# The router's logits in the last stage of a four-stage transformer kernel: the router's columns as the stationary operand, the rows streamed past them, the result copied and turned back

## The reference

```python
logits = jnp.einsum('bsd,ed->bse', x, router_w) + router_b
probs = jax.nn.softmax(logits, axis=-1)
weights = jnp.max(probs, axis=-1)
top1 = jnp.argmax(probs, axis=-1)
y_all = jnp.einsum('bsd,eod->bseo', x, expert_w) + expert_b
y = jnp.take_along_axis(y_all, top1[:, :, None, None], axis=2)[:, :, 0, :]
out = y * weights[:, :, None]
```

## Time and profile before

| | us |
|---|---|
| median of 3 runs | 3087.24 (3087.1 to 3090.45) |
| the profiled execution, its own time | 3084.65 |
| its span | 3082.2 |
| router part of the last stage | some 103, from 2809 to 2912 |
| table and fill rows | some 25, to 2937 |
| tiles | some 145, to the end |

### The profile page before, as it was taken

One profiled execution on the slowest core, in us unless ns is written; L12 is line 12 of the kernel. 1 busy time (PEld: TensorE's weight loads), 2 busy tenths in 40 slices (PEclk: granted clock), 3 DMA queues, 4 the chain that ended last, 5 costly groups with the idle time before them and its releaser, 6 DMA issues. The chain is left out here.

```text
span 3082.2 us, 85861 instructions
## 1 busy us (share of the span) xinstructions
PE 2883.8 (94%) x27000; PEld 2603.0 (84%) x27000; DVE 2280.3 (74%) x6196; ACT 1874.3 (61%) x6944; POOL 1553.2 (50%) x1813
## 2 busy tenths in 40 slices
PE   2999999889999999997999999999989999997777
PEld 2888888689999999996999999999978888886656
DVE  5888888877777777776777777777778888886533
ACT  3888888755555555554444444444378888885443
POOL 1666565566666666665222222222246666563645
PEclk9999999999999999998999999999999999996588
DMA  6000000010000000000000000000010000001243
GB/s 214 15 17 14 17 17 14 2 61 11 10 10 12 10 10 10 10 12 23 25 10 12 12 10 10 10 10 11 1 53 17 14 17 15 15 8 36 94 131 115
DMA packets 55924, 86.12 MB, mean 28 GB/s; under 512 B 6784, under 2 KB 42625, under 8 KB 55042
## 3 DMA queue, kind: packets, MB, share of 16 engines
q1 hardware_dynamic: 47204, 65.69, 6.9%
q0 software_dynamic: 6528, 16.92, 1.5%
q10 hardware_dynamic: 2080, 2.10, 0.2%
HBM read 57.25 MB, written 28.48 MB: 28 GB/s over the span
## 5 line engine op out<-in xcount | busy, mean ns | idle before, releaser
L642 ACT ACTIVATE L_probs<-bank,L_neg_max 128x128 f32<-128x128 f32 x2048 | 716.8, 403 | 138.0 <-DVE L_neg_max L714 137.4
L642 ACT ACTIVATION_READ_ACCUMULATOR L_probs<-bank,L_neg_max 128x1 f32 x2048 | 498.2, 243 | 0.0
L720 DVE COPY L_probsT<-bank 128x512 f32<-128x512 f32 x512 | 352.7, 689 | 141.2 <-PE bank L537 82.3
L1778 ACT ACTIVATE M_inter<-bank 128x512 f32<-128x512 f32 x256 | 153.3, 599 | 438.0 <-PE bank L69 387.1
L67 PE MATMUL bank<-W_hi,M_nT_hi 128*128 128x384 f32 (+1 forms) x1024 | 369.9, 361 | 7.6 <-DVE M_qkv L1404 4.5
L714 DVE TENSOR_REDUCE L_neg_max<-bank 128x4 f32<-128x512 f32 x512 | 327.5, 681 | 36.8 <-PE bank L514 36.8
L69 PE MATMUL bank<-W_lo,M_nT_hi 128*128 128x384 f32 (+1 forms) x1024 | 346.6, 338 | 0.0
L68 PE MATMUL bank<-W_hi,M_nT_lo 128*128 128x384 f32 (+1 forms) x1024 | 346.0, 338 | 0.0
L524 PE MATMUL bank<-constants,L_probs 128*128 128x128 f32 x2048 | 326.0, 283 | 13.0 <-ACT L_probs L642 9.8
L1837 DVE TENSOR_TENSOR M_inter_lo<-M_inter,M_inter_hi 128x512 fp32r<-128x512 f32 x256 | 206.7, 808 | 168.8 <-ACT M_inter_hi L1779 159.7
L67 PE MATMUL bank<-W_hi,M_inter_hi 128*128 128x256 f32 x1024 | 290.4, 284 | 11.7 <-DVE M_inter_lo L1837 10.9
(11 more groups left out here) (344 smaller groups left out, 9232.4 us busy)
## 6 DMA issues: line engine op xcount, KB each, us to landing
L_ctx_in<-in_ctx SPq DMA_DIRECT2D x64, 256.0 KB, 2.6
M_tile<-M_sorted SPq DMA_DIRECT2D x72, 130.0 KB
raw_weights<-in_weights SPq DMA_DIRECT2D x2, 4096.0 KB, 13.5
hs<-M_hs SPq DMA_DIRECT2D x64, 128.0 KB, 1.7
M_hs<-hs SPq DMA_DIRECT2D x32, 256.0 KB, 2.7
x_all<-in_x SPq DMA_DIRECT2D x6, 1024.0 KB, 8.0
M_sorted<-M_fill SPq DMA_DIRECT2D x16, 130.0 KB
x_all<-in_x ACTq DMA_DIRECT2D x2, 1024.0 KB, 14.9
```

Of the source, the lines that this page charges most:

```text
L642: last = act.activation(probs[:, k % UNITS, i, :], score_bank[u][:, i, :], ACT.Exp, bias=neg_max[:, u, i:i + 1], scale=-1.0, accum_out=sum ...
L720: dve.tensor_copy(probsT[:, k % 2], pT_ps[k % UNITS]).then_inc(pT_ready, 1)
L1778: act.activation(inter[:, e % 2], up_bank[e % 2], ACT.Gelu).then_inc(M.inter_ready, 1)
```

## The change

Router products are turned round. `dot_router(p)` now loads the router's columns (16, or 8 for the remainder rows) and streams the 256 tokens of the pair past them, for each half of the features: four products, into [16, 256] of bank 6 or 7. ScalarE copies that into `dotsT` (`keep_dots`). A new step `fold(p)` multiplies, for each of the two sequences, dotsT's 128 tokens (stationary, 16 rows, plain fp32) with a constant [16, 8] of two stacked identities (`fold`, eight columns more in the constants): this turns the dots back to [128 tokens, 8] and adds the two eights. VectorE's first addition of a group falls away. On TensorE `fold(p - 1)` stands between `turn_n(p + 1)` and `dot_router(p)`. The exponential moves from p = 8, 12, ... to p = 9, 13, ... in ScalarE's queue (the first stays at p = 4). `round_n(p)` and `choose(g)` wait for folds where they waited for products.

```diff
--- before.py
+++ after.py
@@ -143,6 +143,7 @@
         "rank": np.tile(np.arange(E, 0, -1), (P, 2, 1)),
         "minus_half": np.full((P, 2), -0.5),
         "one": np.ones((P, 1)),
+        "fold": np.tile(np.eye(E), (P // E, 1)),
         "euler": np.full((P, 2, E), np.e),
     }
 
@@ -1987,7 +1988,8 @@
         sem = lambda name: signals.sem(f"{L}_{name}")
         normed = sb("normed", [P, 2, 2, C])
         nT = [sb("nT_hi", [P, 2, KT, 2 * P], F32R), sb("nT_lo", [P, 2, KT, 2 * P], F32R)]
-        partial, logit, tied, exp, place = (sb(n, [P, GS, E]) for n in ("partial", "logit", "tied", "exp", "place"))
+        dotsT = sb("dotsT", [2 * E, 2, 2 * P])
+        logit, tied, exp, place = (sb(n, [P, GS, E]) for n in ("logit", "tied", "exp", "place"))
         chosen = sb("chosen", [P, NG, GS, E], BF16)
         top, order, total, slot = (sb(n, [P, GS]) for n in ("top", "order", "total", "slot"))
         weight = sb("weight", [P, NG, GS])
@@ -2014,14 +2016,15 @@
         mT = [sb("mT_hi", [P, NT, KT, P], F32R), sb("mT_lo", [P, NT, KT, P], F32R)]
 
         nT_ps = [S.bank[n].rearrange("p (k t) -> p k t", k=KT) for n in range(2)]
-        dots_ps = [S.bank[2 + n][:, 0:GS * 2 * E].rearrange("p (s e) -> p s e", s=GS) for n in range(2)]
+        dotsT_ps = [S.bank[6 + n][0:2 * E, 0:2 * P] for n in range(2)]
+        dots_ps = [S.bank[2 + n][:, 0:GS * E].rearrange("p (s e) -> p s e", s=GS) for n in range(2)]
         place_ps = [S.bank[4 + n][:, 0:GS * E].rearrange("p (s e) -> p s e", s=GS) for n in range(2)]
         count_ps = S.bank[6][:, 0:E]
         mT_ps = [S.bank[n][:, 0:KT * P].rearrange("p (k t) -> p k t", k=KT) for n in (0, 1, 5)]
         y_ps = [S.bank[2 + n][:, 0:C] for n in range(NT)]
         spare = S.bank[7]
 
-        names = ("set bias_loaded bias_rounded bias_split whi_ready wlo_ready shifted meta n_ready tn_ready nhi_ready nlo_ready dots_made dots_read gate_step logits_ready exp_done "
+        names = ("set bias_loaded bias_rounded bias_split whi_ready wlo_ready shifted meta n_ready tn_ready nhi_ready nlo_ready dotsT_made dotsT_kept dots_made dots_read gate_step logits_ready exp_done "
                  "chosen_ready so_far_ready place_made place_step slots_ready weighed count_made table_step table_ready "
                  "scattered scattered_most filled m_ready mT_made mhi_ready mlo_ready y_made y_ready").split()
         M = named(**{n: sem(n) for n in names})
@@ -2064,12 +2067,23 @@
                     last.then_inc(M.tn_ready, 1)
 
                 def dot_router(p):
+
+                    pe.wait_ge(M.nlo_ready, p + 1)
+                    wait(pe, M.dotsT_kept, p - 1)
+                    out = dotsT_ps[p % 2]
+                    for k in range(KT):
+                        pe.matmul(out, R.split[:, k, :], nT[0][:, p % 2, k, :], start=k == 0, stop=False)
+                        last = pe.matmul(out[0:E], R.split[:, k, 0:E], nT[1][:, p % 2, k, :], start=False, stop=k == KT - 1)
+                    last.then_inc(M.dotsT_made, 1)
+
+                def fold(p):
+
                     g = p // GROUP
-                    pe.wait_ge(M.nlo_ready, p + 1)
-                    wait(pe, M.dots_read, 2 * (g - 1))
+                    pe.wait_ge(M.dotsT_kept, p + 1)
+                    wait(pe, M.dots_read, g - 1)
                     for s in range(2):
-                        last = gate_products(pe, dots_ps[g % 2][:, 2 * (p % GROUP) + s, :],
-                                             [[t[:, p % 2, k, s * P:(s + 1) * P] for k in range(KT)] for t in nT], R.split)
+                        last = pe.matmul(dots_ps[g % 2][:, 2 * (p % GROUP) + s, :], dotsT[:, p % 2, s * P:(s + 1) * P],
+                                         S.fold[0:2 * E, :], start=True, stop=True)
                     last.then_inc(M.dots_made, 1)
 
                 def places(g):
@@ -2094,11 +2108,14 @@
                 for p in range(NP):
                     if p + 1 < NP:
                         turn_n(p + 1)
+                    if p:
+                        fold(p - 1)
                     dot_router(p)
                     if p == GROUP:
                         places(0)
                     if p >= 2 * GROUP and p % GROUP == 1:
                         places(p // GROUP - 1)
+                fold(NP - 1)
                 places(NG - 1)
                 pe.wait_ge(M.so_far_ready, NG)
                 pe.matmul(count_ps, ones16[:], so_far16[:, NG - 1, :], start=True, stop=True).then_inc(M.count_made, 1)
@@ -2151,6 +2168,11 @@
                     wait(act, M.dots_made, p - 1)
                     act.activation(nT[0][:, p % 2], nT_ps[p % 2], ACT.Copy).then_inc(M.nhi_ready, 1)
 
+                def keep_dots(p):
+                    act.wait_ge(M.dotsT_made, p + 1)
+                    wait(act, M.dots_made, p - 1)
+                    act.activation(dotsT[:, p % 2], dotsT_ps[p % 2], ACT.Copy).then_inc(M.dotsT_kept, 1)
+
                 def round_w(e):
                     act.activation(W.hi[:, :, e, :], W.raw[:, e], ACT.Copy).then_inc(M.whi_ready, 1)
 
@@ -2160,11 +2182,14 @@
                     if p + 1 < NP:
                         norm(p + 1)
                     round_n(p)
-                    if p % GROUP == 0 and p:
+                    if p:
+                        keep_dots(p - 1)
+                    if p == GROUP or p > 2 * GROUP and p % GROUP == 1:
                         act.wait_ge(M.logits_ready, p // GROUP)
                         act.activation(exp[:], logit[:], ACT.Exp).then_inc(M.exp_done, 1)
                     if 10 <= p < 10 + 2 * E and p % 2 == 0:
                         round_w((p - 10) // 2)
+                keep_dots(NP - 1)
                 act.wait_ge(M.logits_ready, NG)
                 act.activation(exp[:], logit[:], ACT.Exp).then_inc(M.exp_done, 1)
 
@@ -2212,10 +2237,8 @@
 
                     then = chain(M.gate_step, 6 * g)
                     dve.wait_ge(M.dots_made, GROUP * (g + 1))
-                    tt(partial[:], dots_ps[g % 2][:, :, E:2 * E], over(R.bias[:]), ALU.add).then_inc(M.dots_read, 1)
-                    dve.wait_ge(M.dots_read, 2 * g + 1)
-                    tt(logit[:], dots_ps[g % 2][:, :, 0:E], partial[:], ALU.add).then_inc(M.dots_read, 1)
-                    dve.wait_ge(M.dots_read, 2 * g + 2)
+                    tt(logit[:], dots_ps[g % 2], over(R.bias[:]), ALU.add).then_inc(M.dots_read, 1)
+                    dve.wait_ge(M.dots_read, g + 1)
                     then(dve.tensor_reduce(top[:], logit[:], AX.X, ALU.max))
                     then(tt(tied[:], logit[:], wide(top), ALU.is_ge))
                     then(tt(tied[:], tied[:], over(S.rank[:, 0, :]), ALU.mult))
@@ -2441,7 +2464,7 @@
         S.constants = sb("constants", [P, sum(widths)])
         c = dict(zip(shapes, parts(S.constants, widths)))
         S.ident, S.hidden, S.head_half, S.minus_half = c["ident"], c["hidden"], c["head_half"], c["minus_half"]
-        S.one = c["one"]
+        S.one, S.fold = c["one"], c["fold"]
         S.hide_q16, S.hide_k16, S.rest_q16, S.rest_k16, S.rest_count_k16, S.before16 = (
             c[n].bitcast(BF16) for n in ("hide_q", "hide_k", "rest_q", "rest_k", "rest_count_k", "before"))
         S.region, S.token, S.tiles = c["region"], c["token"], c["tiles"]
```

## The result

The changed kernel took 3093.64 us (median of 17 runs, 3090.79 to 3098.26), the kernel before 3090.21 beside it (17 runs, 3087.1 to 3093.37): ratio of the runs 1.0016, 95% interval 1.0009 to 1.0023. That is slower by 3.4 us by the medians and by 5 by the ratio. The forecast was 3078, 9 us faster, with a range up to 3090. The interval leaves no doubt that the change costs something, though less than the 0.2% that the prediction takes as the least that can be told.

What follows compares the result with a forecast made beforehand. TensorE's work and waits in the router part were taken to bound: five groups from 12.6 to 10.8 save 9.0 us, the first interval gains about 1, the last loses 1.0. From the 3087.24 median: 3078, range 3064 to 3090.

Steps and rivals of the forecast that it cites:

- the second wait: Behind a group's places, VectorE and ScalarE start late on the transposes, idling TensorE 0.53 us; the forecast kept 0.3.
- the pair of 2.30 us: TensorE's work per pair of sequences: 0.75 + 0.85 + 0.85 - 0.15 = 2.30 us, against 2.46 before.
- the 0.15 taken off for the next transpose's load: On TensorE, the next transpose's load runs under the last router product, saving 0.15 us a pair (between 0 and 0.19).
- 16 rows but again 128 columns: TensorE's folds, with dotsT stationary, cost 0.214 us a pass, four passes a pair: 0.85 us.
- Rival B: No change that can be told: the load doesn't hide or a fold pass costs 0.25 us; 3083 us, chance 0.28.
- The copy: ScalarE's 32 copies of the dots out of PSUM: 0.38 us each, covered by TensorE's pair.
- Exp: Moving ScalarE's exp from pair 4g to 4g+1 takes away its 2.93 us of waiting for VectorE's logits.
- They lie beside the chain: GpSimd's 64 scatters, 1.25 us each, waited 34.9 us for slots, so they were held not to lengthen the router part.
- Ahead of the first slots, put at nothing: The sum covered only the seven intervals between the eight slot vectors, 87.2 us, with no change before the first.
- rival C: Slower: the way products, copy, fold between TensorE and ScalarE takes 0.6 us more per pair; 3097 us, chance 0.10.
- (D): TensorE's clock rises to 2.4 GHz in the router part, a group falling to 9.2 us; 3067 us, chance 0.12.
- VectorE's wait for a fold before choose: choose waits for the group's last fold, so TensorE stands about 1.0 us per group in place of the first wait.

Runs made afterwards that it cites:

- the padded kernel: Changed kernel with dotsT on 128 rows, rows 16 to 127 zero: 3046.51 against 3056.75 us for the kernel before; a second time 3089.49 against 3089.97.
- run 6: Kernel before with only ScalarE's exp moved from pair 4g to 4g+1: 3049.87 against 3056.75 us on one chip, 3085.87 against 3083.5 (1.0003) a second time.
- run 9: Changed kernel with round_n waiting for the products instead of the fold: 1.0012 of the kernel before with 16 rows, 0.9993 with 128 rows.
- run 8: Unaltered changed kernel and kernel before, measured again with profiles on one chip: 3095.88 against 3089.97 us.
- the 64-row kernel: Changed kernel with dotsT on 64 rows instead of 16: 3059.94 against 3059.75 us for the kernel before, one run.
- trains of four: Changed kernel with 128-row dotsT; GpSimd issues four of each group's eight scatters at once, the others after the last slots: groups 8.8 to 9.8 us.

## Why the prediction was wrong

Two steps failed, and each alone would have undone the forecast: the second wait, of which the sum kept 0.3 us (there is a floor under the group), and the pair of 2.30 us (it is 2.77). With the pair mended and the floor there, nothing is gained (128 rows, 12.7 to 14.0 a group). With the floor away and the pair as it is, nothing is gained either (11.8 against 11.7, and 3059.94 against 3059.75).

- **Pair, 2.30.** Measured 2.77. The counts and slots were right: four products 0.84 (forecast 0.85), four passes 0.22 each (0.214). A small part of the error is the 0.15 taken off for the next transpose's load: the 0.75 of the earlier trace rows held some of that already. Twelve slots of 0.214 are 2.57; the forecast took 0.27 off, and the padded kernel shows 0.20. The rest is the folds' 16 rows, which the text took as harmless ("16 rows but again 128 columns"): they cost 0.4 us a pair around the folds, which no row read beforehand shows. With 128 rows the pair is 2.37, the forecast plus 0.07. Rival B, a dearer pass at 0.25, comes nearest, but it is not the pass that was dearer: two of them saved 0.44.
- **ScalarE.** The copy took 0.37 (forecast 0.38), and in a steady pair it was hidden, as forecast.
- **Exp.** Gone as forecast, and worth 1.3 us a group where nothing else holds it (run 6).
- **The second wait of the earlier trace rows, "I keep 0.3".** This is the step that decided on the chips with the lag, the one of the prediction's trace among them. The lag was read as a fixed delay of TensorE's signals, of which some is paid. It was the end of the scatter train, which sets a floor of 12.6 to 12.8 us under a group on these chips. "They lie beside the chain", and the 34.9 us that GpSimd waited, were read as room; the loop runs through GpSimd's train, 8.84 us from its first start to its last, and the 2.7 behind that. Of the 34.9, 22.3 stood ahead of the first two trains; in the five middle groups GpSimd waited 2.4 to 2.8 each, which is the loop's own rest. All five intervals of before, 12.6 to 12.7, were already at the floor (the exp move alone shows it, 12.5 to 12.7): nothing taken off TensorE or ScalarE could show.
- **Ahead of the first slots, put at nothing.** The sum counts from the first slots on. The pairs ahead of them are dearer too, and no train runs there: 15.9 us became 17.5, in the profile at 0.50.
- **Why slower, then.** The sum of the intervals grew by 5.4 us: 1.9 in the last (copy and fold exposed, and four dearer pairs; forecast 1.0), 0.5 in the first, and 3.0 in the middle, of which the two long intervals (13.9 for 12.7, 14.0 for 12.6) make 2.6. Those are round_n's: the change moved its release from the products to the fold, one slot later, where the lag strikes it (run 9). The text of the change costed the copy's wait and choose's, and overlooked this third one, whose semaphore has the same name in both kernels. That the lag could strike dotsT's signal, as rival C had it, came too (the rows at 2902.32), and that group took 12.8 like those beside it. A fold's signal can come late while the train still runs: at 2899.53, ahead of the last scatter, ScalarE's round_n goes on 1.6 us after the fold that it waited for is recorded as ended.
- **Clock.** 0.50 in the profiled run, as forecast, but that was partly luck: in the second profile of the same kernel three pairs ahead of the first slots ran at 1.00, as (D) had it, and saved 3.9 us there (run 8). Among the slots, (D) came in stretches once the folds had 128 rows or one pass.
- **VectorE's wait for a fold before choose** came as forecast; groups that hold it still take 12.8. From the waits of the changed kernel between its first and last slots (total, times, longest):

```profile
DVE M_logit L2240 <- PE bank L2085: 10.4, 6, 3.5
```

Added up from the traces, the change costs 1.6 ahead of the first slots, 0.5, 3.0 and 1.9 between them: 7.0 us; with the 3.0 less behind the last slots, 4.0. The runs say 3.4 by the medians and 5 by the ratio. This is an account of what was measured, not what the prediction's method would have given. By the size of the change the case that came is nearest to (B), but it is a loss, not a smaller gain, and by a reason that was not among its two.

What stays open: what holds these signals while the train drains, why others sent in the same train pass (the steady pairs beside it take 2.77), and what makes a run one of the kind without the lag. Also open: the unpadded changed kernel without the lag was not run (the 64-row kernel stands for it), and how much of the padded kernel's 10 us is the clock's is not known.

The best version is the changed kernel with dotsT on 128 rows and round_n off the fold: 0.9965 of the kernel before on the chips without the lag; with it 0.9993, an interval that includes 1.

## What to carry to other kernels

Before costing a saving, find the loop that sets the period which it should shorten. Five intervals within 0.1 us, in a stage whose engines all wait a little, ask for that, but don't answer it: without the train the intervals were as even, at 11.7, and another loop set them. Add up each loop through every engine, the one that "has room" and the wait behind its DMAs too; a saving beside the longest is worth nothing. A run that takes the suspected loop away, as the held-back scatters here, tells which it is. When a wait is moved to another event, look for every other wait on the same semaphore. And where products of different kinds alternate on TensorE, try the same number of rows for all, with zeros if need be: here it was 0.4 us for each visit of four passes with 16 or 64 rows.

## What the hardware did that I had not expected

- A stationary side of 16 or 64 rows between ones of 128 costs 0.14 us ahead of it, 0.22 up to the products behind it and 0.03 behind those, at a granted clock of 0.50 (pairs of 2.77 and 2.37 us, otherwise the same).
- In one kind of runs, signals sent behind the places arrive 1.9 to 2.8 us after the start of the last scatter of a train, up to 4.3 us after the instruction that sends one was recorded as ended. With no scatters, or trains of four, no such wait is left. In the other kind of runs there was none at all. The same program is 31 us shorter there, 24 of them behind the last slots, in the table, the fill rows and the tiles.
- Zero rows that do no useful work went with a higher granted clock: windows of 0.74 and 1.00 between the first and the last slots, where the kernel with 16 rows stood at 0.50 in both its profiles. The one-pass folds, without such rows, had it too (0.69), so the rows are not the only way to it.
